# The bias of the last product enters through a gated modulation row, and ScalarE instead of VectorE empties the product's two banks

## The chip, the core and the metric

The kernel runs on one core of a Trainium2 chip. Five engines work side by side, each through its own list of instructions in order, and wait for each other on semaphores: TensorE (PE in the profile; PEld is its weight load), VectorE (DVE), ScalarE (ACT), GpSimd (POOL) and SyncE (SP), which here issues the DMAs. The metric is the device time of one launch in microseconds (us); lower is better.

## The reference

The whole is one transformer block with adaptive layer norm, over 32 batches of 512 tokens with 256 features. Cut to what matters here:

```python
mod = (silu(c) @ wmod).reshape(B, 6, 1, -1)
sa, ca, ga, sb, cb, gb = (mod[:, i] for i in range(6))
ga, gb = ((2*(g >= 0) - 1) * maximum(abs(g), 0.25) for g in (ga, gb))
h  = layernorm(x) * (1 + ca) + sa
x  = x + ga * attn_and_ssm(h)        # softmax attention + a selective scan + an FFN
h  = layernorm(x) * (1 + cb) + sb
x  = x + gb * (h @ base_w.T + base_b + 2.0 * lora_of_top2_experts(h))
```

`attn_and_ssm` is attention with 16 heads, beside it a state-space scan (512 channels times 16 states, over the 512 tokens), then an FFN with GELU. The last line is the one that the change touches: a product, a bias `base_b`, a gate `gb`, and the residual.

## The kernel before, in words

A batch of 512 tokens is four tiles of 128. The scan of a batch is 64 steps `e`, each over a 128x512 tile: ScalarE makes the decay (`dec`, L695), GpSimd fills the state (`fill`, L582), VectorE scans (`scan`, L1173), VectorE or GpSimd multiplies by C (`c`, L1181; `pc`, L569), TensorE adds it up in PSUM (`add`, L914). The states lie in a ring of eight, the rows of B and C come by DMA (`bc`, L436) into four slots. Between these stands the other work of three batches at once: the next batch's layer norm, projections and convolution (names with + in the tables), this batch's attention, the last batch's tail (names with -).

Four tables, ORDER["POOL"], ORDER["ACT"], ORDER["DVE"] and ORDER["PE"], and one for SP, write out by hand in which order each engine takes its steps in one turn of the loop. `drive` runs the table once per batch: 32 turns, the first two and last two outside the loop. Nothing is scheduled at run time: an engine waits at a step until its semaphores are there, and what stands behind waits too.

The steps that the prediction follows, in the order of one turn:

- `x2`, `x2b` on GpSimd (L623, L626): the second residual `xr` = x + ga * (...), a 128x1024 tile in SBUF. SP has loaded `xr`, the two gate rows `mod_g` (L504) and `mod_f` for it.
- `l3s` on VectorE and GpSimd, `l3a` on ScalarE (L702): the layer norm of `xr`. GpSimd then goes on with `fill27` to `fill31`, and `fill32` to `fill35` as soon as the next row of B is in.
- `ql0` to `ql3` on VectorE (L1210): the third bfloat16 part of Q and K of the next batch. Both inputs, `dbc` (the tile `qkf`) and the part before, lie in SBUF. The first two of four run beside `fill27` to `fill31`.
- `route` and `lora` on VectorE: the top-2 weights. `lora` has two small instructions with both inputs in SBUF (L1308, L1314), then L1319, from which TensorE's transposes `axt` (L923) take the lora part.
- `out0`, `out1` on TensorE (L1094, L1096): the last product, into PSUM banks 3 and 1; VectorE adds the bias row `bb_row` and writes SBUF (L1326). TensorE's `st0_3_0` needs bank 3 next, `mx1_6` bank 1.
- `mx1_4` to `mx1_10` (L1235): the maxima of attention scores on VectorE; `mx1_4` and `mx1_5` use the same bank 0, so TensorE starts `mx1_5` (L1002, L1004) when VectorE has read `mx1_4`. They end in `mt1`, whose result goes by DMA to the scores of the next group of heads.
- `gb` and `put` on GpSimd (L632, L635): times the gate row, plus `xr`.

The eviction before reads:

```python
v.tensor_tensor(nrm(b)[:, 2*n:2*n+2], pM[...] , bb_row (broadcast), ALU.add)   # DVE
nc.gpsimd.tensor_tensor(nrm(b), nrm(b), row(mod_g[:, 1, :]), ALU.mult)         # gb
nc.gpsimd.tensor_tensor(nrm(b), nrm(b), xr, ALU.add)                           # put
```

Of the kernel before, what the change touches and what calls it, by code (L numbers as in the profile page):

```python
# [1345 lines left out]
def parse(text):  # L1346
# [14 lines left out]
        fill40 fill41 pc38 fill42 fill43 pc39 fill44 fill45 fill46 fill47 fill48 fill49 fill50 fill51 pc46 pc47
        fill52 fill53 fill54 fill55 fill56 fill57 fill58 fill59 pc54 fill60 fill61 pc55 fill62 fill63 +u0 +u1
        +fill0 +fill1 pc62 pc63 +fill2 +fill3 +fill4 +fill5 +fill6 +fill7 +fill8 +fill9 +pc6 +pc7 +fill10 +fill11
        +fill12 +fill13 l2s +fill14 +fill15 +fill16 +fill17 +pc14 f1_0 +fill18 +pc15 +fill19
# [94 lines left out]
```

## Time and profile before

| | us |
|---|---|
| three runs | 6279.98, 6290.32, 6291.08 |
| their median | 6290.32 |
| the profiled execution | 6288.11, its span 6286.3 |
| VectorE busy | 5319.2 (85%) |
| TensorE busy, granted clock | 5399.8 (86%), 0.94 |
| GpSimd busy | 4141.0 (66%) |
| ScalarE busy | 4051.5 (64%) |

A turn of the loop takes 181 to 196 us. A timeline row gives the start in us from the beginning of the span, the length, the engine, the line, the operation with output and inputs, how many instructions are merged in it, and in square brackets how long the engine had been idle before and what ended that. Inputs are named once: `region<-region` may be two tiles of the region. Ends of TensorE's matmuls are modelled.

### The profile page before, as it was taken

Reading aid. Unit: us, or ns where it says so; the run is one execution under the profiler, and the core shown is the slowest. Engines: PE = TensorE matmul, PEld = TensorE weight load, DVE = VectorE, ACT = ScalarE, POOL = GpSimd, SP = SyncE. Lnnn points to the kernel's source line nnn. Section 1 sums busy time; section 2 is a strip of 40 time slices with the busy share of each in tenths; the row PEclk is TensorE's granted clock in tenths of the full one; section 3 lists DMA queues with packets and bytes.
Section 4 is the critical chain, followed back from the end, with each engine's and each line's share of the span. In section 5 each row is a group of like instructions: output and inputs, shape, how many; then the busy total and the mean of one; then the engine's idle time right before and its main releaser. Section 6 shows DMA issues by size and latency. Waiting matters only on the chain.

```text
span 6286.3 us, 116694 instructions
## 1 busy us (share of the span) xinstructions
PE 5399.8 (86%) x32280; PEld 3560.7 (57%) x32280; DVE 5319.2 (85%) x8095; ACT 4051.5 (64%) x6215; POOL 4141.0 (66%) x3409
## 2 busy tenths in 40 slices
PE   4788988888888888888888888888888989888986
PEld 2455655556555565555565555565555655555664
DVE  4888889888899888898888898888898888988883
ACT  3666766666666666766666666667766667666663
POOL 3666676667676676676666666676766666766762
PEclk7899999999999999999999999999999999999998
DMA  4443444444444444444434444434444444444331
GB/s 123 137 128 120 135 130 143 137 122 131 132 134 135 133 126 129 134 138 132 138 120 125 127 148 135 124 125 134 132 138 135 125 125 132 141 130 140 123 117 44
DMA packets 517124, 810.56 MB, mean 129 GB/s; under 512 B 79921, under 2 KB 222681, under 8 KB 516369
## 3 DMA queue, kind: packets, MB, share of 16 engines
q1 hardware_dynamic: 508464, 801.56, 41.4%
q8 instruction: 297, 4.87, 0.3%
q14 instruction: 459, 3.75, 0.2%
q10 hardware_dynamic: 7904, 0.39, 0.1%
...
## 4 chain that ended last, share of the span: by engine, by line
PE 34%; DVE 21%; issue 19%; POOL 9%; ACT 9%; DMA 5%; SPq 2%; ACTq 1%; DVEq 1%; POOLq 0%
PE pM L1065 7%; DVE pD L1173 5%; PE pY L914 5%; PE pM L1056 4%; DMA region<-mrow 4%; POOL state L582 4%; PE pM L1020 3%; DVE mx L1235 3%; ACT pD L695 3%; PE pM L1002 3%; DVE xc L1217 2%; DVE state L1173 2%; PE pM L936 2%; DVE state L1181 2%; PE pM L923 2%
## 5 line engine op out<-in xcount | busy, mean ns | idle before, releaser
L582 POOL TENSOR_TENSOR state<-scan_in,bc 128x512 f32<-128x512 f32 x2048 | 2586.0, 1287 | 894.3 <-PE pY L914 469.2
L1173 DVE TENSOR_TENSOR_SCAN pD<-pD,state 128x512 f32<-128x512 f32 x1536 | 1851.1, 1218 | 194.9 <-ACT pD L695 179.0
L695 ACT ACTIVATE pD<-scan_in,A 128x512 f32<-128x512 f32 x2048 | 1401.6, 689 | 641.8 <-DVE state L1181 547.8
L914 PE MATMUL pY<-ident,state 128*128 128x128 f32 x8192 | 1217.6, 285 | 94.8 <-DVE state L1181 72.1
L796 ACT ACTIVATE region<-pM 128x512 f32<-128x512 f32 (+1 forms) x1408 | 747.9, 555 | 639.7 <-PE pM L1022 619.2
L914 PEld LDWEIGHTS pY<-ident,state 128*128 128x128 f32 x8192 | 954.0, 147 | 286.2 <-issue 106.6
L1181 DVE TENSOR_TENSOR state<-pD,bc 128x512 f32<-128x512 f32 x1536 | 1032.5, 681 | 27.2 <-DMA bc<-bc_d 0.4
L1235 DVE TENSOR_REDUCE mx<-pM 128x1 f32<-128x512 f32 (+3 forms) x1408 | 863.9, 628 | 125.2 <-PE pM L1004 98.2
L569 POOL TENSOR_TENSOR state<-state,bc 128x512 f32<-128x512 f32 x512 | 645.6, 1272 | 390.9 <-DVE state L1173 390.0
L1020 PE MATMUL pM<-region 98*128 98x512 bf16 (+3 forms) x2048 | 594.5, 339 | 327.1 <-DMA region<-mrow 198.8
L1002 PE MATMUL pM<-region 96*128 96x512 bf16 (+3 forms) x2048 | 553.5, 316 | 166.9 <-DVE mrow L1248 44.7
L1173 DVE TENSOR_TENSOR_SCAN state<-pD,state 128x512 f32<-128x512 f32 x512 | 605.9, 1209 | 56.4 <-ACT pD L695 56.3
L1020 PEld LDWEIGHTS pM<-region 98*128 98x128 bf16 x2048 | 210.9, 103 | 641.5 <-ACT region L796 165.6
L1056 PE MATMUL pM<-region,w_f 128*128 128x512 f32 x1024 | 479.8, 606 | 21.2 <-ACT region L820 21.2
L1065 PE MATMUL pM<-w_f,scan_in 128*128 128x256 f32 x2048 | 455.7, 381 | 5.7 <-ACT scan_in L829 5.7
L1002 PEld LDWEIGHTS pM<-region 96*128 96x128 bf16 x2048 | 205.1, 101 | 438.3 <-issue 218.2
L1022 PE MATMUL pM<-identb,mask_qk 128*128 128x128 bf16 x2048 | 430.4, 237 | 0.0
L1065 PEld LDWEIGHTS pM<-w_f,scan_in 128*128 128x128 f32 x2048 | 385.3, 191 | 60.4 <-ACT scan_in L829 6.5
L936 PE MATMUL pM<-region,vt 128*17 128x512 f32 (+3 forms) x4096 | 383.8, 465 | 19.9 <-issue 18.8
L1004 PE MATMUL pM<-mask_qk,identb 128*128 128x128 bf16 x2048 | 400.0, 225 | 0.0
L611 POOL TENSOR_TENSOR scan_in<-scan_in,xc 128x1024 f32<-128x1024 f32 x64 | 149.5, 2357 | 250.2 <-DVE scan_in L1224 244.4
L1056 PEld LDWEIGHTS pM<-region,w_f 128*128 128x128 f32 x1024 | 182.0, 191 | 211.1 <-issue 165.4
...
## 6 DMA issues: line engine op xcount, KB each, us to landing
...
region<-qk_d SPq DMA_DIRECT2D x256, 64.0 KB, 2.3
...
```

The lines of the kernel that those rows point to most:

```text
L569: nc.gpsimd.tensor_tensor(slot, slot, bc[:, e // JP % BC_SLOTS, 1, :], ALU.mult).then_inc(pp_ok.sem, 1)
L582: nc.gpsimd.tensor_tensor(state[:, e % RING], us[:, parity(b), k // N * JP + e % JP, :], bc[:, k % BC_SLOTS, 0, :], ALU.mult).then_inc(b_o ...
L695: act.activation(pD[DECAY_BANK[e]][:], dts[:, parity(b), j], ACT.Exp, scale=A[:, j, n:n + 1]).then_inc(a_ok.sem, 1)
L796: act.activation(probs[kb % 2][:, h:h + heads, 0:n], pM[bank_of(name)][:, 0:heads * n].rearrange("p (h t) -> p h t", h=heads), ACT.Exp, sc ...
L914: ins = pe.matmul(y_part(t, e % JP), state[:, e % RING, t * P:(t + 1) * P], ident[:], is_transpose=True, start=False, stop=(e % PASS >= PA ...
L1002: pe.matmul(ps[:, s * n:(s + 1) * n], q[0:QK_ROWS, h, qb * P:(qb + 1) * P], kk[0:QK_ROWS, h, 0:n], start=True, stop=False, skip_group_chec ...
L1020: pe.matmul(ps[:, i * n:(i + 1) * n], kk[0:QK_ROWS + 2, h + i, kb * P:(kb + 1) * P], q[0:QK_ROWS + 2, h + i, kb * P:L], start=True, stop=F ...
L1056: ins = pe.matmul(ps[:], w_f1[:, k, f * P:(f + 1) * P], h2T[:, k], start=(k == 0), stop=(k == KT - 1))
L1065: ins = pe.matmul(ps[:, t * D:(t + 1) * D], gT(b)[:, f, (2 * n + t) * P:(2 * n + t + 1) * P], w_f2[:, f, :], start=(f == 0), stop=(f == FT ...
L1173: v.tensor_tensor_scan(h if e in POOL_C else decay, decay, h, 0.0, ALU.mult, ALU.add)\
L1181: v.tensor_tensor(state[:, e % RING], pD[DECAY_BANK[e]][:], bc[:, slot, 1, :], ALU.mult)\
L1235: v.tensor_reduce(mx[:, g % 2].rearrange("p (h q) -> p h q", q=TB)[:, heads[0]:heads[-1] + 1, qb], pM[bank_of(name)][:, 0:len(heads) * n]. ...
```

## The change

The bias is taken out of the eviction: gb * (p + base_b) = gb * p + gb * base_b. In the set-up VectorE makes gb * base_b for all 32 batches as a seventh modulation row beside the six. In each turn SP loads that row as a third of `mod_g` (one DMA more, 128 KB), and GpSimd adds it to `xr` in a new step `xb`, behind the layer norm that reads `xr`. The two evictions of the last product become plain copies on ScalarE. The tables change in four places: `-xb` behind `fill28` on GpSimd, `-out0 -out1` behind `dec33` on ScalarE, the same two names gone from VectorE; TensorE's and SP's tables stay.

```diff
-        mod_rows = dram("mod_rows", (B, 6 * D))
+        mod_rows = dram("mod_rows", (B, 7 * D))
...
-                    for a, col in ((0, 2), (1, 5)):
+                    for a, col in ((0, 2), (1, 5), (2, 6)):
                         sp.dma_start(mod_g[:, a], mod_rows[b.index, col * D:(col + 1) * D].partition_broadcast(P))\
                           .then_inc(modg_in.sem, 16)
...
+                elif name == "xb":
+
+                    b.wait(pool, n3)
+                    nc.gpsimd.tensor_tensor(xr, xr, row(mod_g[:, 2, :]), ALU.add).then_inc(xb_ok.sem, 1)
...
                 elif name == "put":
                     b.wait(pool, o_gb)
+                    b.wait(pool, xb_ok)
...
+                elif name in ("out0", "out1"):
+                    n = int(name[3])
+                    b.wait(act, out_ps, n + 1)
+                    act.activation(nrm(b)[:, 2 * n:2 * n + 2], pM[bank_of(name)][:].rearrange("p (t f) -> p t f", t=2),
+                                   ACT.Copy).then_inc(o_sum.sem, 1)
...
+            dve.wait_ge(bb_in, 16)
+            link(v.tensor_tensor(mods[0:B, 6 * D:7 * D], mods[0:B, 5 * D:6 * D], bb_row[0:B], ALU.mult))
...
-                elif name in ("out0", "out1"):
-                    n = int(name[3])
-                    b.wait(dve, out_ps, n + 1)
-                    v.tensor_tensor(nrm(b)[:, 2 * n:2 * n + 2], pM[bank_of(name)][:].rearrange("p (t f) -> p t f", t=2),
-                                    bb_row[:].unsqueeze(1).broadcast_to([P, 2, D]), ALU.add)\
-                     .then_inc(o_sum.sem, 1)
...
-        fill28 fill29 fill30 fill31 fill32 fill33 fill34 fill35 pc30 pc31 fill36 -gb fill37 -put fill38 fill39
+        fill28 -xb fill29 fill30 fill31 fill32 fill33 fill34 fill35 pc30 pc31 fill36 -gb fill37 -put fill38
...
-        dec31 st0_2_2 dec32 dec33 st0_3_0 dec34 dec35 st1_0_0 st1_0_1 dec36 st1_0_2 oe0 dec37 st1_0_3 st1_1_0
+        dec31 st0_2_2 dec32 dec33 -out0 -out1 st0_3_0 dec34 dec35 st1_0_0 st1_0_1 dec36 st1_0_2 oe0 dec37 st1_0_3
```

GpSimd, from the small instructions of the layer norm of `xr` on. Before:

```order
L549 TENSOR_TENSOR ln_rs<-ln_mv,eps 128x4
L550 TENSOR_TENSOR ln_nm<-ln_mv,mone 128x4
L552 TENSOR_TENSOR ln_rs<-ln_rs,mhalf 128x4
L555 TENSOR_TENSOR ln_nm<-ln_nm,ln_rs 128x4
L582 TENSOR_TENSOR state<-scan_in,bc 128x512 x9
L569 TENSOR_TENSOR state<-state,bc 128x512 x2
```

Changed:

```order
L551 TENSOR_TENSOR ln_rs<-ln_mv,eps 128x4
L552 TENSOR_TENSOR ln_nm<-ln_mv,mone 128x4
L554 TENSOR_TENSOR ln_rs<-ln_rs,mhalf 128x4
L557 TENSOR_TENSOR ln_nm<-ln_nm,ln_rs 128x4
L584 TENSOR_TENSOR state<-scan_in,bc 128x512 x2
L634 TENSOR_TENSOR region<-region 128x1024
L584 TENSOR_TENSOR state<-scan_in,bc 128x512 x7
L571 TENSOR_TENSOR state<-state,bc 128x512 x2
```

The 128x1024 add `xb` now stands between the second and the third of the nine fills.

VectorE, from the last instruction of `lora` to the scan of step 33. Before:

```order
L1319 TENSOR_TENSOR scan_in<-pM,top 128x512
L1181 TENSOR_TENSOR state<-pD,bc 128x512
L1173 SCALAR_TENSOR_TENSOR pD<-pD,state 128x512
L1181 TENSOR_TENSOR state<-pD,bc 128x512
L1173 SCALAR_TENSOR_TENSOR state<-pD,state 128x512 x2
L1173 SCALAR_TENSOR_TENSOR pD<-pD,state 128x512
L1326 TENSOR_TENSOR scan_in<-pM,bb_row 128x512
L1181 TENSOR_TENSOR state<-pD,bc 128x512
L1235 TENSOR_REDUCE mx<-pM 128x1
L1326 TENSOR_TENSOR scan_in<-pM,bb_row 128x512
L1235 TENSOR_REDUCE mx<-pM 128x1
L1173 SCALAR_TENSOR_TENSOR pD<-pD,state 128x512
```

Changed:

```order
L1333 TENSOR_TENSOR scan_in<-pM,top 128x512
L1195 TENSOR_TENSOR state<-pD,bc 128x512
L1187 SCALAR_TENSOR_TENSOR pD<-pD,state 128x512
L1195 TENSOR_TENSOR state<-pD,bc 128x512
L1187 SCALAR_TENSOR_TENSOR state<-pD,state 128x512 x2
L1187 SCALAR_TENSOR_TENSOR pD<-pD,state 128x512
L1195 TENSOR_TENSOR state<-pD,bc 128x512
L1249 TENSOR_REDUCE mx<-pM 128x1 x2
L1187 SCALAR_TENSOR_TENSOR pD<-pD,state 128x512
```

The two evictions are gone, and the maxima `mx1_4` and `mx1_5` follow one another directly.

ScalarE, from the eviction of `axt`. Before:

```order
L841 ACTIVATE scan_in<-pM 128x512
L695 ACTIVATE pD<-scan_in,A 128x512
L796 ACTIVATE region<-pM 128x2x256
L695 ACTIVATE pD<-scan_in,A 128x512
L796 ACTIVATE region<-pM 128x2x256
L695 ACTIVATE pD<-scan_in,A 128x512 x2
L796 ACTIVATE region<-pM 128x4x128
L695 ACTIVATE pD<-scan_in,A 128x512 x2
```

Changed:

```order
L853 ACTIVATE scan_in<-pM 128x512
L702 ACTIVATE pD<-scan_in,A 128x512
L803 ACTIVATE region<-pM 128x2x256
L702 ACTIVATE pD<-scan_in,A 128x512
L803 ACTIVATE region<-pM 128x2x256
L702 ACTIVATE pD<-scan_in,A 128x512 x2
L849 ACTIVATE scan_in<-pM 128x512 x2
L803 ACTIVATE region<-pM 128x4x128
L702 ACTIVATE pD<-scan_in,A 128x512 x2
```

The two evictions stand ahead of the exponential of `st0_3_0` (128x4x128).

## Rows read from the trace of the kernel before

**Rows 1.** Busy us by stretch: one turn, from `x2b` to L1319, and its rest.
```profile
core 0: us, PE busy (x) PEld busy (x) DVE busy (x) ACT busy (x) POOL busy (x), PEclk, DMA share, GB/s
2843.90:2867.80 23.90, 20.86 (x114) 12.25 (x113) 20.19 (x43) 13.03 (x24) 12.37 (x12) 1.00 0.47 154
2867.80:3031.40 163.60, 145.15 (x895) 97.92 (x896) 145.86 (x210) 113.31 (x171) 116.83 (x96) 0.95 0.42 131
```

**Rows 2.** Timeline of VectorE around the two evictions, in that turn.
```profile
2873.06 1.21 DVE L1173 TENSOR_TENSOR_SCAN pD<-pD,state 128x512 f32<-128x512 f32 x1
2874.18 0.67 DVE L1326 TENSOR_TENSOR scan_in<-pM,bb_row 128x512 f32<-128x512 f32 x1
...
2875.83 0.68 DVE L1326 TENSOR_TENSOR scan_in<-pM,bb_row 128x512 f32<-128x512 f32 x1
2876.42 0.55 DVE L1235 TENSOR_REDUCE mx<-pM 128x1 f32<-128x384 f32 x1
```

**Rows 3.** Timeline of TensorE there: end of `out1`, then `mx1_5`.
```profile
2874.98 0.59 PE L1096 MATMUL pM<-w_lb,scan_in 128*128 128x256 f32 x2
2875.96 0.34 PE L1002 MATMUL pM<-region 96*128 96x384 bf16 x1 [0.39 <-DVE mx L1235]
2876.14 0.22 PE L1004 MATMUL pM<-mask_qk,identb 128*128 128x128 bf16 x1
```

**Rows 4.** Timeline of ScalarE there: the exponential of `st0_3_0`.
```profile
2877.22 0.60 ACT L796 ACTIVATE region<-pM 128x512 f32<-128x512 f32 x1 [3.35 <-PE pM L1022]
```

**Rows 5.** Timeline of ScalarE at `l3a`, same turn.
```profile
2850.31 1.57 ACT L702 ACTIVATE scan_in<-region,ln_nm,ln_rs 128x256 f32<-128x256 f32 x3
```

**Rows 6.** Timeline of GpSimd, same turn: `fill28`, `fill32` to `fill35`, `gb`.
```profile
2850.96 1.72 POOL L582 TENSOR_TENSOR state<-scan_in,bc 128x512 f32<-128x512 f32 x1
...
2866.32 4.98 POOL L582 TENSOR_TENSOR state<-scan_in,bc 128x512 f32<-128x512 f32 x4 [9.51 <-DMA bc<-bc_d]
...
2879.68 2.35 POOL L632 TENSOR_TENSOR scan_in<-scan_in,region 128x1024 f32<-128x1024 f32 x1
```

**Rows 7.** Timeline of VectorE, same turn: `ql0`, `ql1`, `ql2`, `ql3`, end of `lora`.
```profile
2849.91 1.64 DVE L1210 TENSOR_TENSOR qkp<-dbc,qkp 128x512 bf16<-128x512 f32 x1
...
2854.71 0.97 DVE L1210 TENSOR_TENSOR ht<-dbc,ht 128x512 bf16<-128x512 f32 x1 [0.19 <-ACT ht L743]
...
2858.17 0.68 DVE L1210 TENSOR_TENSOR qkp<-dbc,qkp 128x512 bf16<-128x512 f32 x1
...
2865.44 0.68 DVE L1210 TENSOR_TENSOR ht<-dbc,ht 128x512 bf16<-128x512 f32 x1
...
2867.75 0.69 DVE L1319 TENSOR_TENSOR scan_in<-pM,top 128x512 f32<-128x512 f32 x1
```

**Rows 8.** Timeline of GpSimd in another turn: `fill32`.
```profile
2292.07 1.57 POOL L582 TENSOR_TENSOR state<-scan_in,bc 128x512 f32<-128x512 f32 x1 [8.88 <-DMA bc<-bc_d]
```

**Rows 9.** Timeline of VectorE in the turn of rows 8: `ql3` and `lora`.
```profile
2291.82 0.68 DVE L1210 TENSOR_TENSOR ht<-dbc,ht 128x512 bf16<-128x512 f32 x1
2292.42 1.27 DVE L1308 TENSOR_TENSOR top<-top,keep 128x32 f32<-128x32 f32 x1
...
2294.16 0.76 DVE L1314 SCALAR_TENSOR_TENSOR top<-top,esum 128x32 f32<-128x32 f32 x1
2295.02 0.69 DVE L1319 TENSOR_TENSOR scan_in<-pM,top 128x512 f32<-128x512 f32 x1
```

**Rows 10.** Two lines of VectorE, whole span: busy us, mean ns | idle before.
```profile
L1314 DVE SCALAR_TENSOR_TENSOR top<-top,esum 128x32 f32<-128x32 f32 x32 | 25.6, 801 | 1.1
...
L1308 DVE TENSOR_TENSOR top<-top,keep 128x32 f32<-128x32 f32 x32 | 10.4, 324 | 3.9 <-ACT top L838 3.9
```

**Rows 11.** Timeline of SP: the two gate rows of a turn.
```profile
3014.35 0.87 SPq L504 DMA_DIRECT2D region<-mod_rows  x2
```

**Rows 12.** Timeline of GpSimd: `x2` of that turn.
```profile
3028.94 2.36 POOL L623 TENSOR_TENSOR scan_in<-x,region 128x1024 f32<-128x1024 f32 x1 [7.13 <-DVE x L1283]
```

**Rows 13.** Who waited for SP's DMA of the split parts (L456): us, times.
```profile
  ACT qkp L738: 6.9, 5
```

More of the change, by code:

```diff
@@ L215, in adaln_block @@
         lns = [stats_tiles(f"ln{n}") for n in range(4)]
-        REGION = 12288
+        REGION = 12544
         region = sb("region", [P, REGION])
@@ L239, in adaln_block @@
         xr = view(TB * D).rearrange("p (t f) -> p t f", t=TB)
-        mod_g = view(2 * D).rearrange("p (a f) -> p a f", a=2)
+        mod_g = view(3 * D).rearrange("p (a f) -> p a f", a=3)
         def gT(b):
@@ L265, in adaln_block @@
         rt_raw = view(D)
-        mods = view(6 * D)
+        mods = view(7 * D)
+        bb_row = view(D)
         alpha = view(D)
@@ L345, in adaln_block @@
         la_ps, ax_ok, axt_ps, axt_ok = sig("la_ps", 1), sig("ax_ok", 1), sig("axt_ps", 1), sig("axt_ok", 1)
+        xb_ok = sig("xb_ok", 1)
         out_ps, o_sum, o_gb, o_fin, out_done = (sig("out_ps", 2), sig("o_sum", 2), sig("o_gb", 1),
@@ L409, in _ @@
             load(A[:], d["A_log"].rearrange("(j p) n -> p j n", p=P))
-            for row, name in ((ob_row, "o_b"), (f2b_row, "ffn_b2"), (bb_row, "base_b"), (rb_row, "router_b")):
+            for row, name in ((ob_row, "o_b"), (f2b_row, "ffn_b2"), (rb_row, "router_b")):
                 load(row[:], d[name].partition_broadcast(P))
@@ L1335 @@
              + [(1, [0, 1]), (1, [2, 3]), (0, [0, 1, 2, 3])])
-N_LOADS = 39
+N_LOADS = 38
 ACT_LOADS = 22
@@ L1339 @@
 BUILT = 11
-MODS_READY = 14
+MODS_READY = 15
 MODS_DONE = MODS_READY + 1
@@ L1359 @@
         +l0s fill20 fill21 +l0a fill22 +l0b fill23 +l0c fill24 +l1s fill25 pc22 fill26 pc23 -x2 -x2b -l3s fill27
-        fill28 fill29 fill30 fill31 fill32 fill33 fill34 fill35 pc30 pc31 fill36 -gb fill37 -put fill38 fill39
[L1361 to L1364, printed above, removed]
+        fill28 -xb fill29 fill30 fill31 fill32 fill33 fill34 fill35 pc30 pc31 fill36 -gb fill37 -put fill38
+        fill39 fill40 fill41 pc38 fill42 fill43 pc39 fill44 fill45 fill46 fill47 fill48 fill49 fill50 fill51 pc46
+        pc47 fill52 fill53 fill54 fill55 fill56 fill57 fill58 fill59 pc54 fill60 fill61 pc55 fill62 fill63 +u0
+        +u1 +fill0 +fill1 pc62 pc63 +fill2 +fill3 +fill4 +fill5 +fill6 +fill7 +fill8 +fill9 +pc6 +pc7 +fill10
+        +fill11 +fill12 +fill13 l2s +fill14 +fill15 +fill16 +fill17 +pc14 f1_0 +fill18 +pc15 +fill19
     """,
@@ L1396 @@
         mx1_0 +l1s scan23 scan24 c24 scan25 -f2_0 scan26 -f2_1 c25 -l3s +qk0 mx1_1 +ql0 mx1_2 scan27 +qk1 c26
-        +ql1 +qk2 scan28 c27 +ql2 mx1_3 -route +xs0 +qk3 +xs1 +ql3 -lora c28 scan29 c29 scan30 scan31 scan32
-        -out0 c32 mx1_4 -out1 mx1_5 scan33 mx1_6 c33 mx1_7 mx1_8 mx1_9 mx1_10 mt1 scan34 mx2_0 gate0 c34 scan35
-        c35 scan36 scan37 c36 mx2_1 c37 on0 scan38 scan39 mx2_2 scan40 mx2_3 c40 scan41 mx2_4 scan42 c41 c42
-        mx2_5 mx2_6 +xs2 mx2_7 mx2_8 mx2_9 mx2_10 scan43 mt2 c43 +xs3 scan44 mx3_0 scan45 mx3_1 c44 mx3_2 on1 c45
-        mx3_3 scan46 scan47 mx3_4 scan48 c48 mx3_5 scan49 scan50 mx3_6 c49 mx3_7 c50 mx3_8 scan51 scan52 c51
-        mx3_9 mx3_10 c52 mt3 scan53 c53 scan54 +mx0_0 scan55 scan56 scan57 c56 c57 scan58 scan59 c58 c59 on2 +sp3
-        scan60 c60 scan61 c61 scan62 scan63 +scan0 +scan1 +c0 +c1 on3 gate1 +scan2 +c2 +scan3 +scan4 +c3 +c4
-        +scan5 +c5 +scan6 +scan7 +scan8 +c8 +scan9 +c9 +scan10 +c10 sso0 +scan11 +c11 sso1 l2s +scan12 +scan13
-        +c12 +mx0_1 +mx0_2 +c13 +scan14 +mx0_3 +scan15 +mx0_4 +scan16 +c16 +scan17
+        +ql1 +qk2 scan28 c27 +ql2 mx1_3 -route +xs0 +qk3 +xs1 +ql3 -lora c28 scan29 c29 scan30 scan31 scan32 c32
+        mx1_4 mx1_5 scan33 mx1_6 c33 mx1_7 mx1_8 mx1_9 mx1_10 mt1 scan34 mx2_0 gate0 c34 scan35 c35 scan36 scan37
+        c36 mx2_1 c37 on0 scan38 scan39 mx2_2 scan40 mx2_3 c40 scan41 mx2_4 scan42 c41 c42 mx2_5 mx2_6 +xs2 mx2_7
+        mx2_8 mx2_9 mx2_10 scan43 mt2 c43 +xs3 scan44 mx3_0 scan45 mx3_1 c44 mx3_2 on1 c45 mx3_3 scan46 scan47
+        mx3_4 scan48 c48 mx3_5 scan49 scan50 mx3_6 c49 mx3_7 c50 mx3_8 scan51 scan52 c51 mx3_9 mx3_10 c52 mt3
+        scan53 c53 scan54 +mx0_0 scan55 scan56 scan57 c56 c57 scan58 scan59 c58 c59 on2 +sp3 scan60 c60 scan61
+        c61 scan62 scan63 +scan0 +scan1 +c0 +c1 on3 gate1 +scan2 +c2 +scan3 +scan4 +c3 +c4 +scan5 +c5 +scan6
+        +scan7 +scan8 +c8 +scan9 +c9 +scan10 +c10 sso0 +scan11 +c11 sso1 l2s +scan12 +scan13 +c12 +mx0_1 +mx0_2
+        +c13 +scan14 +mx0_3 +scan15 +mx0_4 +scan16 +c16 +scan17
     """,
```

16 lines of the change are left out of this document (8 added, 8 removed).

## The prediction

> **What bounds the kernel now.** I read the busy times by stretch first. From `x2b` to the end of `lora` a turn has VectorE busy for 20.19 of 23.90 us, and in the rest for 145.86 of 163.60 us; TensorE has as much [rows 1]. Neither is the bound alone: each waits now for the other. So the next view is the timeline of both where the change cuts. VectorE goes from the scan of step 32 to the first eviction, on to `mx1_4`, the second eviction and `mx1_5` without a pause [rows 2], and TensorE waits 0.39 us for VectorE's `mx1_4` before it can start `mx1_5` [rows 3]. ScalarE has 3.35 us of idle time before `st0_3_0` [rows 4]. GpSimd has 9.51 us before `fill32`, in which it waits for a row of B [rows 6]. Taken by idle time alone the change looks free: work leaves the engine that is waited for and goes to two that are waiting. The view that says otherwise is the length of single VectorE instructions while GpSimd works, below.
>
> **What leaves VectorE.** Two evictions, 0.67 and 0.68 us long, the next instruction 0.59 us behind the start [rows 2]: 1.2 us a turn, on an engine without a pause there. Not all of it is won. Without them the product of step 32 starts when its scan ends, 2873.06 + 1.21 = 2874.3, `mx1_4` about 0.6 later at 2874.9, and it ends (0.55 long, like `mx1_5`) at 2875.45. But `mx1_5` uses the same bank, and TensorE is in `out1` until 2875.5 to 2875.6 (2874.98 + 0.59 is the modelled end [rows 3]). So TensorE becomes the late one: `mx1_5` starts there at 2875.55 and is complete 0.40 us later (2876.14 + 0.22 - 2875.96), and VectorE reads it at 2875.95 instead of 2876.42 [rows 2, 3]. **The gain is 0.5 us a turn**; the other 0.7 us becomes a wait of VectorE for TensorE. From there to `mt1` VectorE has no slack, so the 0.5 us should reach the scores of the next heads: 30 turns x 0.5 = **15 us**.
>
> **What ScalarE gets.** Two copies of a 128x512 bank, by the eviction in rows 4 about 0.6 us each. The first bank is full long before, the second at 2875.57, so the second copy ends near 2876.2. TensorE's `st0_3_0`, which was complete shortly before 2877.22, comes 0.45 us earlier, at about 2876.75. So both copies lie in the 3.35 us of idle time and cost nothing; were the cover gone, one copy would cost 0.6 us a turn, 18 us in all. Behind them stand that exponential and the decays of steps 34 and 35, which VectorE reads some us later.
>
> **What SP gets.** One more DMA issue, 0.87 / 2 = 0.43 us, at 3015.2, and SP's later `mod_f` as much later. GpSimd's `x2` starts at 3028.94, and the last thing that it waited for was VectorE [rows 11, 12]. Even a landing 10 us after issue comes before that: nothing. In the set-up one small VectorE product of 32x256 is added and one DMA moves forward: between 0.2 us (a 32-wide instruction less its stall) and 0.7 us (a 512-wide one, rows 7), I take 0.5 us, once.
>
> **What GpSimd gets.** `xb` is a 128x1024 add, 2.35 us like `gb` [rows 6]. It waits for `l3a`, which ends at 2850.31 + 1.57 = 2851.9, before `fill28` ends at 2852.68 [rows 5, 6]: no wait. What is queued behind it are `fill29` to `fill31`, each 2.3 us later; nobody needs them early (`scan29` comes after `lora`), and `fill32` still waits for its DMA. On GpSimd's own account: nothing.
>
> Now the same turn with `xb`: it starts at 2852.64 and ends at 2854.99. `ql1`, asked for at 2854.71, ends at 2855.54 (before: 2855.68). `fill29` is held by it until 2855.54 + 1.14 = 2856.68, and fills follow at 1.24 us ((4.98 - 1.27) / 3 in rows 6, with 1.27 for one alone): `fill30` from 2856.64 and `fill31` from 2857.88 to 2859.15. `ql2` comes at 2858.17 [rows 7], when before the fills had been over for 1.4 us (`fill31` began at 2855.09). It is now held, and ends at 2859.15 + 0.55 = 2859.70 instead of 2858.85: **+0.85 us**. From here to L1319 VectorE is back to back, and so it hands this on.
>
> That delay brings `ql3` from 2865.44 to 2866.3, where `fill32` starts at 2866.32, set by a DMA that the delay doesn't touch. This is the pattern of [rows 8, 9]: there L1319 starts 3.20 us after `ql3`, here it was 2.31 [rows 7, 9]. On average before, L1308 and L1314 lose 0.14 and 0.61 us (324 and 801 less 0.18 and 0.19 unheld) = 0.75; in the pattern 1.09 + 0.57 = 1.66 us: **+0.9 us**. Together 1.75 us a turn. It holds for the turns in which `ql2` comes while `fill31` runs, I count 26 of 30; in the others Q's first DMA landed late (ScalarE waited for it five times [rows 13]), and `ql2` comes after the fills even now. 26 x 1.75 = 45 us. In some turns `fill32` starts just before `ql3`; then `ql3` is held too and L1319 loses another 1.15 us; I take four such turns, 5 us. **The loss is 50 us.** Ends: 26 x 0.85 = 22 us if only `ql2` is hit, 26 x 2.9 = 75 us if `fill32` is always first.
>
> The Trainium skill states this as a rule (SBUF — State Buffer, "Who interferes with whom"): a VectorE instruction with two SBUF inputs and a GpSimd instruction that reads SBUF need one shared port pair, and the one that comes second waits for the whole instruction. By that rule, the trace agrees: 1.64 against 0.68 us. By a rule in which GpSimd costs VectorE nothing the sum would be 6288 - 15.
>
> **The sum.** 6288.1 (the profiled execution) - 15 + 50 + 0.5 = 6323.6. The median of the runs is 2.2 above the profiled execution: **6325 us** (rounded).
>
> **Rivals.**
> (a) The meeting of `ql2` and `fill31` doesn't happen or is made up later. For it: it hangs on an offset of 0.3 us into `fill31`, and TensorE and ScalarE have idle time too. Against it: the turns repeat to a few hundredths, and VectorE shows no pause until `mt1`. Then only the gain is left: 6290 - 15 = 6275. It decides as soon as `ql2` comes 1 us later than now.
> (b) The whole 1.2 us is won and nothing is lost, because TensorE's modelled end of `out1` is too late: 6290 - 30 x 1.2 = 6254.
> (c) Only the first meeting costs, since `lora` finds `fill32` elsewhere: 6290 - 15 + 22 = 6297, no change.
> (d) TensorE's longer wait ahead of `axt` (it follows L1319) costs clock as well. The granted clock is 1.00 in the stretch before and 0.95 over the rest [rows 1]; were it half in the 7 us from `axt` to `out1`, each turn would lose up to 3.5 us, 100 us at most; I put one turn in five at half of that, 10 us, in the range and not in the sum. With it and (c)'s upper end: over 6350.
> (e) The change doesn't do what it says, since ScalarE, now in VectorE's place, is late for the banks: it has `dec33` in front, which waits for the scan of step 31. That scan ends before the one of step 32, so a copy can't start later than VectorE's did; even then 6290.
>
> **How the numbers follow.** Chances: the forecast (6303 to 6350) 0.60, (a) 0.12, (b) 0.04, (c) 0.14, (d) above 6350 0.06, (e) 0.04. Range: from (a), 6273, to 6350; (b) and (d) are left out. About 0.2% (12.6 us) is what a measurement of this kernel can tell from no change. Faster by more: (a) and (b), 0.16; within: (c) and (e), 0.18; slower: 0.66.
>
> **What would show it.** In the changed profile the third L1210 of a turn takes about 1.6 us instead of 0.68 in most turns; L1308's mean rises from 0.32 towards 1.2 us; L1326's line is gone and VectorE waits about 0.6 us for TensorE before `mx1_5`; ScalarE's idle time before `st0_3_0` shrinks; `xb` starts right behind `fill28`. If the third L1210 is still 0.68 us long, the loss isn't there and the time is (a)'s. If it is 1.6 and the time is still no more than before, the delay was made up behind `lora`, and my step from VectorE's timeline to the span is wrong.

## The result and the profile after

| | before | changed |
|---|---|---|
| median of the runs, us | 6290.7 (6279.98 to 6305.84, 6 runs) | 6351.03 (6336.21 to 6366.26, 6 runs) |
| profiled execution, its span | 6288.11, 6286.3 | 6349.76, 6348.0 |
| ratio of changed to before, 95% interval | | 1.0097 [1.0078, 1.0116] |

The changed kernel is slower by 60 us (49 to 73 by the interval), where 35 were forecast. The direction and the main mechanism were right, the size was not, and the time lies 1 us above the range.

First the groups of instructions of VectorE in the changed kernel: line, operation, out<-in, count | busy us, mean ns of one | idle before, and who ended it. L1224 is L1210 of before, L1322 and L1328 are L1308 and L1314, L1333 is L1319, L1249 is L1235, L584 is L582, L634 is the new `xb`.

```profile
L1249 DVE TENSOR_REDUCE mx<-pM 128x1 f32<-128x384 f32 x512 | 275.0, 542 | 46.9 <-PE pM L1016 25.8 <-issue 20.3
...
L1224 DVE TENSOR_TENSOR qkp<-dbc,qkp 128x512 bf16<-128x512 f32 x64 | 98.7, 1542 | 1.4 <-ACT qkp L750 1.4
...
L1322 DVE TENSOR_TENSOR top<-top,keep 128x32 f32<-128x32 f32 x32 | 35.2, 1100 | 3.8 <-ACT top L845 3.8
...
L1328 DVE SCALAR_TENSOR_TENSOR top<-top,esum 128x32 f32<-128x32 f32 x32 | 23.5, 734 | 1.1
```

The same groups of before:

```profile
L1235 DVE TENSOR_REDUCE mx<-pM 128x1 f32<-128x384 f32 x512 | 274.4, 541 | 23.7 <-issue 19.8 <-PE pM L1004 3.1
...
L1210 DVE TENSOR_TENSOR qkp<-dbc,qkp 128x512 bf16<-128x512 f32 x64 | 73.0, 1141 | 1.4 <-ACT qkp L743 1.4
```

Half of the `qkp` instructions are `ql0`, which stays at 1.65 us; the other half, `ql2`, went up: 64 x (1542 - 1141) / 32 = 0.80 us more a turn. L1322 went from 324 to 1100 ns, L1328 from 801 to 734 [rows 10]. And in front of the 384-wide maxima, `mx1_5` among them, VectorE now waits 25.8 us for TensorE instead of 3.1.

Now one turn of the changed kernel, the same as that of [rows 2 to 7]. GpSimd, from `fill27` to `fill31`:

```profile
2889.89 2.95 POOL L584 TENSOR_TENSOR state<-scan_in,bc 128x512 f32<-128x512 f32 x2
2892.80 2.36 POOL L634 TENSOR_TENSOR region<-region 128x1024 f32<-128x1024 f32 x1
2895.12 4.17 POOL L584 TENSOR_TENSOR state<-scan_in,bc 128x512 f32<-128x512 f32 x3
```

VectorE at the same time: `ql1`, and `ql2`:

```profile
2894.88 0.83 DVE L1224 TENSOR_TENSOR ht<-dbc,ht 128x512 bf16<-128x512 f32 x1 [0.20 <-ACT ht L750]
...
2898.26 1.58 DVE L1224 TENSOR_TENSOR qkp<-dbc,qkp 128x512 bf16<-128x512 f32 x1
```

`xb` starts right behind `fill28`. The fills are over at 2895.12 + 4.17 = 2899.29, and `ql2`, asked for at 2898.26, ends at 2899.84, 0.55 us behind them. It was 0.68 us long in [rows 7]. Then GpSimd's `fill32` and VectorE's `ql3` and `lora`:

```profile
2906.30 2.94 POOL L584 TENSOR_TENSOR state<-scan_in,bc 128x512 f32<-128x512 f32 x2 [7.01 <-DMA bc<-bc_d]
```

```profile
2906.43 1.68 DVE L1224 TENSOR_TENSOR ht<-dbc,ht 128x512 bf16<-128x512 f32 x1
2908.03 1.25 DVE L1322 TENSOR_TENSOR top<-top,keep 128x32 f32<-128x32 f32 x1
...
2909.76 0.75 DVE L1328 SCALAR_TENSOR_TENSOR top<-top,esum 128x32 f32<-128x32 f32 x1
2910.61 0.69 DVE L1333 TENSOR_TENSOR scan_in<-pM,top 128x512 f32<-128x512 f32 x1
```

Here `fill32` is 0.13 us before `ql3`: the worse of the two patterns of the prediction, in which `ql3` is held as well. L1333 starts 26.56 us behind `x2b` (at 2884.05); before it was 23.9 [rows 1, 7].

What follows in this turn, TensorE:

```profile
2911.36 0.66 PE L935 MATMUL pM<-ident,scan_in 128*128 128x128 f32 x4 [2.65 <-DVE scan_in L1333]
...
2913.15 1.91 PE L1106 MATMUL pM<-w_base,region 128*128 128x256 f32 x4
...
2917.12 1.08 PE L1106 MATMUL pM<-w_base,region 128*128 128x256 f32 x4
```

The second and the third row are four matmuls each, of one shape, in `out0` and in `out1`: they take 1.91 us the first time and 1.08 the second. Busy us by stretch, from `x2b` to L1333 and from there to `mt1`; the granted clock stands behind the parenthesis of POOL:

```profile
core 0: us, PE busy (x) PEld busy (x) DVE busy (x) ACT busy (x) POOL busy (x), PEclk, DMA share, GB/s
2884.05:2910.62 26.57, 21.13 (x114) 12.18 (x113) 22.79 (x43) 12.95 (x24) 17.39 (x14) 1.00 0.48 150
2910.62:2925.80 15.18, 13.71 (x100) 11.01 (x101) 12.75 (x18) 7.27 (x12) 7.31 (x6) 0.89 0.18 51
```

Behind a wait of 2.65 us, TensorE ran for 3.4 us of the second stretch at 1.2 GHz, half of its 2.4 (0.11 lost of 15.18 us is 1.7, so 3.4 at half). This is rival (d).

To see where 62 us of span go, I took the start of `x2b`, of L1319 (L1333) and of `mt1` from the timelines of all 28 turns between the first two and the last two, and made the means. They are of one execution of each kernel:

| us a turn | before | changed | difference | forecast |
|---|---|---|---|---|
| `x2b` to L1319 | 24.00 | 25.77 | +1.77 | +1.67 (50 / 30) |
| L1319 to `mt1` | 14.19 | 14.06 | -0.13 | -0.50 |
| `mt1` to the next `x2b` | 152.21 | 152.65 | +0.44 | 0 |
| whole turn | 190.40 | 192.48 | +2.08 | +1.17 |

30 turns x 2.08 = 62 us, the whole difference of the two spans. The loss was well sized; most of the gain is missing, and the stretch behind `mt1` came on top. How far that last row can be trusted is said further down.

### The profile page after: what moved, and what is told of

The parts are those of the page before. It is cut to its first block, busy times and chain, and to the rows that moved or that the text cites. A ratio compares the mean times of both kernels' runs of the same rounds, so it can differ in the third digit from the quotient of the medians.

```text
span 6348.0 us, 116848 instructions
## 1 busy us (share of the span) xinstructions
PE 5417.2 (85%) x32280; PEld 3571.8 (56%) x32280; DVE 5341.6 (84%) x8032; ACT 4086.0 (64%) x6279; POOL 4224.2 (67%) x3441
## 4 chain that ended last, share of the span: by engine, by line
PE 36%; DVE 19%; issue 19%; POOL 9%; ACT 9%; DMA 5%; SPq 2%; ACTq 1%; DVEq 0%; POOLq 0%
PE pM L1077 7%; PE pY L926 5%; PE pM L1068 4%; DVE pD L1187 4%; POOL state L584 4%; DMA region<-mrow 4%; PE pM L1032 3%; PE pM L1014 3%; DVE xc L1231 2%; ACT pD L702 2%; DVE mx L1249 2%; PE pM L948 2%; PE pM L1106 2%; DVE state L1187 2%; DVE state L1195 2%
## 5 line engine op out<-in xcount | busy, mean ns | idle before, releaser
L584 POOL TENSOR_TENSOR state<-scan_in,bc 128x512 f32<-128x512 f32 x2048 | 2596.0, 1291 | 864.1 <-PE pY L926 534.9
L1249 DVE TENSOR_REDUCE mx<-pM 128x1 f32<-128x512 f32 (+3 forms) x1408 | 864.6, 629 | 145.3 <-PE pM L1016 117.1
```

The costliest lines, as they stand in the source:

```text
L584: nc.gpsimd.tensor_tensor(state[:, e % RING], us[:, parity(b), k // N * JP + e % JP, :], bc[:, k % BC_SLOTS, 0, :], ALU.mult).then_inc(b_o ...
L1249: v.tensor_reduce(mx[:, g % 2].rearrange("p (h q) -> p h q", q=TB)[:, heads[0]:heads[-1] + 1, qb], pM[bank_of(name)][:, 0:len(heads) * n]. ...
```

## The experiments

All ratios are to the kernel before, run on the same chip beside them, with 95% intervals. Its median there was 6288.82 us for e1 to e4, 6290.93 for e5 to e8 and 6290.23 for e9 to e11, so kernels of different groups are compared by their ratios. "Changed" is the kernel of the diff. Times of a part of the turn are means of 28 turns, worked out as in the table above.

**Each half of the change alone.** The first kernel is the kernel before with ScalarE in VectorE's place for the two evictions; there is no bias, no `xb` and no seventh row. The second is the changed kernel with the evictions back on VectorE, as copies.

```diff
# e1, against before
-        dec31 st0_2_2 dec32 dec33 st0_3_0 dec34 dec35 ...
+        dec31 st0_2_2 dec32 dec33 -out0 -out1 st0_3_0 dec34 dec35 ...
-        -out0 c32 mx1_4 -out1 mx1_5 scan33 ...
+        c32 mx1_4 mx1_5 scan33 ...
# e2, against changed
-        dec31 st0_2_2 dec32 dec33 -out0 -out1 st0_3_0 dec34 dec35 ...
+        dec31 st0_2_2 dec32 dec33 st0_3_0 dec34 dec35 ...
-        ... scan31 scan32 c32 mx1_4 mx1_5 scan33 ...
+        ... scan31 scan32 -out0 c32 mx1_4 -out1 mx1_5 scan33 ...
```

> The kernel before with one part of the change: ScalarE evicts the last product, behind dec33, as a plain copy. No seventh row, no xb; the bias is left out of the computation. Theory A (the changed kernel is slower only because GpSimd's xb makes the fills meet VectorE's third L1210): L1319 stays at 24.0 us behind x2b, the stretch from L1319 to mt1 is 0.36 us shorter as in the changed kernel, and the time is 6291 - 30 x 0.36 = 6280. Theory B (the 0.45 us a turn that came behind mt1 are ScalarE's doing): the stretch from mt1 to the next x2b is longer by that, and the time is 6290 or more.

> The changed kernel with the evictions given back to VectorE, as plain copies at their old places; the seventh row, its DMA and xb stay. Theory A: the third L1210 takes 1.58 us, L1319 comes 1.77 us later, nothing is won behind it: 6291 + 30 x 1.77 = 6344, and if what came behind mt1 is a consequence of the delay too, up to 6365. Theory B: 6344 or less, and the stretch behind mt1 is as in the kernel before.

Measured: e1 6279.77 us, ratio 0.9992 [0.9982, 1.0001], with 13.83 us from L1319 to `mt1` instead of 14.19; e2 6356.21 us, 1.0117 [1.01, 1.0134], with 25.96 us from `x2b` to L1319 instead of 24.00, and with 14.67 us from there to `mt1`, since 11 of its 28 turns are at half clock there. VectorE in e2:

```profile
L1219 DVE TENSOR_TENSOR qkp<-dbc,qkp 128x512 bf16<-128x512 f32 x64 | 99.3, 1552 | 1.4 <-ACT qkp L750 1.4
...
L1317 DVE TENSOR_TENSOR top<-top,keep 128x32 f32<-128x32 f32 x32 | 36.6, 1143 | 3.8 <-ACT top L845 3.8
```

All of the loss comes with `xb`, all of the gain with the evictions. And the gain is 0.36 us a turn, 11 us, not 15. In the time of the whole kernel it isn't clear of noise: e1's interval reaches 1.

**`xb` out of VectorE's way, or VectorE out of `xb`'s.** e3 is the changed kernel with `xb` behind `pc31`; e4 leaves `xb` where it is and puts `ql2` behind `mx1_3` and `route`, after the fills; e7 puts `xb` behind `fill31`, so that `ql2` meets `xb` itself and not a fill.

```diff
# e3, against changed
-        fill28 -xb fill29 fill30 fill31 fill32 fill33 fill34 fill35 pc30 pc31 fill36 -gb ...
+        fill28 fill29 fill30 fill31 fill32 fill33 fill34 fill35 pc30 pc31 -xb fill36 -gb ...
# e4, against changed
-        ... scan28 c27 +ql2 mx1_3 -route +xs0 ...
+        ... scan28 c27 mx1_3 -route +ql2 +xs0 ...
# e7, against changed
-        fill28 -xb fill29 fill30 fill31 fill32 ...
+        fill28 fill29 fill30 fill31 -xb fill32 ...
```

> The changed kernel with xb moved on GpSimd's table from behind fill28 to behind pc31, ahead of fill36, where GpSimd waited 3.9 us for TensorE and VectorE reads PSUM. Theory A: the third L1210 is 0.68 us again, L1319 at 24.0 us, gain of 0.36 us a turn kept: 6280. Rival (any 2.3 us of added GpSimd work costs, since GpSimd is late for the ring behind it): fill36 and what follows come later, the scans of steps 36 to 38 wait, and it stays above 6300.

> The changed kernel with one swap on VectorE's table: the third L1210 (ql2) stands behind mx1_3 and route instead of ahead of them, so it is asked for about 1.6 us later, when fill31 is over; GpSimd's order stays as changed. Theory A: it takes 0.68 us, L1319 is back at about 24.0 us, and the time is 6280. Rival (the fills that come 2.3 us later hurt by themselves, whatever VectorE meets): still about 6350.

> The changed kernel with xb behind fill31 instead of behind fill28. No fill is late any more, but xb itself now runs from 12.9 to 15.2 us behind x2b, when the third L1210 comes at 14.3. Theory A (what counts is only that GpSimd is reading SBUF when VectorE asks for two SBUF inputs): the third L1210 takes 1.6 us, L1319 comes 1.7 us late, 6350. Rival (what counts is that the fills are late): 0.68 us and 6280.

Measured: e3 6278.02 us, 0.9988 [0.9974, 1.0002]; e4 6281.96 us, 0.9996 [0.9983, 1.0009]; e7 6350.46 us, 1.0092 [1.0075, 1.0108]. In the turn of the traces above `ql2` is short in e3 and e4 and held in e7. First e3:

```profile
2861.83 0.68 DVE L1224 TENSOR_TENSOR qkp<-dbc,qkp 128x512 bf16<-128x512 f32 x1
```

Then e4, where it stands behind the `route` instructions:

```profile
2868.15 0.68 DVE L1224 TENSOR_TENSOR qkp<-dbc,qkp 128x512 bf16<-128x512 f32 x1
```

And e7, GpSimd's `xb` and VectorE's `ql2`:

```profile
2890.33 2.35 POOL L634 TENSOR_TENSOR region<-region 128x1024 f32<-128x1024 f32 x1
```

```profile
2891.73 1.50 DVE L1224 TENSOR_TENSOR qkp<-dbc,qkp 128x512 bf16<-128x512 f32 x1
```

`xb` ends there at 2892.68 and `ql2` at 2893.23, 0.55 us behind it, just as behind a fill. So what costs isn't `xb`'s time on GpSimd, its DMA or its place in a queue; it is that `ql2` is asked for while GpSimd adds, be it a fill or `xb`. e4 has exactly the GpSimd work of the changed kernel and is faster by 1.0097 - 0.9996 = 1.0%, 63 us, by one name that moved on VectorE. And with `ql2` free, L1308's mean stays near before's too (357 ns in e3, 404 in e4, against 1100): the second meeting, of `lora` with `fill32`, is a consequence of the first.

**Does it take a read?** e11 is e3 with a `memset` of GpSimd on an unused 128x2048 bfloat16 view of `x1` behind `fill31`, so that `ql2` meets an instruction that writes SBUF and reads nothing. SP's next load of `x1` waits for the memset.

```diff
# e11, against e3
-                    b.wait_last(sp, x2_ok, 1)
+                    b.wait_last(sp, ms_ok)
                     sp.dma_start(x1[:], hres_d[b.index].rearrange("(t p) f -> p t f", p=P)).then_inc(x1p_in.sem, 16)
...
+                elif name == "ms":
+                    nc.gpsimd.memset(x1_f.bitcast(BF16), 0.0).then_inc(ms_ok.sem, 1)
-        fill28 fill29 fill30 fill31 fill32 ...
+        fill28 fill29 fill30 fill31 -ms fill32 ...
```

> The kernel with xb behind pc31, and a GpSimd memset of 128x2048 bfloat16 (about 1.8 us, into a dead tile) behind fill31: it writes SBUF and reads nothing, and runs from 12.9 to 14.7 us behind x2b, when the third L1210 comes at 14.3. Theory A (only GpSimd's reading of SBUF holds a VectorE instruction with two SBUF inputs): the third L1210 stays at 0.68 us, and the time is that without the memset, 6278. Rival (any GpSimd instruction that uses SBUF holds it): it takes about 0.95 us, and L1319 comes 0.3 to 1.2 us later, 6290 to 6315.

Measured: 6288.13 us, 0.9995 [0.9983, 1.0007]. GpSimd and VectorE in the same turn:

```profile
2855.80 1.81 POOL L638 MEMSET x<- 128x2048 bf16 x1
```

```profile
2857.22 0.68 DVE L1228 TENSOR_TENSOR qkp<-dbc,qkp 128x512 bf16<-128x512 f32 x1
```

The memset runs until 2857.61, `ql2` is asked for at 2857.22 and takes its 0.68 us. Had it been held, it would have ended at 2857.61 + 0.55 = 2858.16; it ends at 2857.90. In 29 turns `ql2` starts during the memset, and their mean is 0.68 us. The Trainium skill states this limit (SBUF — State Buffer, "Who interferes with whom"): a two-input VectorE instruction contends with a GpSimd instruction that reads SBUF, and not with one that only writes. By that rule, the trace agrees. The overlap here is only the last 0.4 us of the memset; an overlap with its start wasn't tried. The time of the kernel doesn't decide between the two theories: its median is 10 us above e3's, near the rival's 6290, but the intervals of the two ratios overlap (e3's is 0.9974 to 1.0002). The length of `ql2` decides it.

**Why the gain is 0.36 us and not more.** The prediction let `mx1_5` wait for the end of `out1`. e5 was to make `out1` earlier: it lets TensorE do `st0_2_2` and `add27` before `axt`, in the time in which it waits for L1333 anyway. e6 does the same to the changed kernel, e8 to the kernel before. e9 instead lets VectorE do other work between `mx1_4` and `mx1_5`.

```diff
# e5 against e3, e6 against changed, e8 against before
-        ... pv0_0 pv0_1 -axt st0_2_2 add27 -out0 mx1_4 -out1 mx1_5
+        ... pv0_0 pv0_1 st0_2_2 add27 -axt -out0 mx1_4 -out1 mx1_5
# e9, against e3
-        ... scan31 scan32 c32 mx1_4 mx1_5 scan33 mx1_6 c33 ...
+        ... scan31 scan32 mx1_4 c32 scan33 mx1_5 mx1_6 c33 ...
```

> The changed kernel with xb behind pc31 and, on TensorE's table, st0_2_2 and add27 moved from behind axt to ahead of it, where TensorE waits for L1319 (0.80 us on average). It tests why only 0.36 of the 1.2 us of the evictions is won. Theory A (TensorE's chain axt, st0_2_2, add27, out0, out1 is what mx1_5 then waits for): with 0.85 us less in that chain, the stretch from L1319 to mt1 shrinks from 13.83 to 13.2 us, and the time is 6278 - 30 x 0.6 = 6260. Rival (VectorE's chain itself, through c32 and the maxima, allows no more): it stays at 6278.

> The changed kernel, xb left behind fill28, with the same swap on TensorE's table alone. TensorE's wait ahead of axt falls from 1.86 us on average to 1.0. Theory A (in five of 28 turns a wait of more than about 2.4 us there took the clock down for out0 and out1, which cost 1.3 to 1.5 us each): no turn between L1319 and mt1 at half clock any more, 0.23 us a turn, and 0.6 us from the shorter chain: 6351 - 30 x 0.8 = 6327. Rival: the swap gives only the 0.6 us, and the half clock stays: 6333.

> The kernel before with the swap on TensorE's table alone. Theory A: before, VectorE is the later one at mx1_5 (out1 was complete 0.26 us ahead of the second eviction), so a TensorE that is 0.85 us earlier wins nothing: 6289. Rival (TensorE's chain sets the pace there in any case): 6289 - 30 x 0.6 = 6271.

> The changed kernel with xb behind pc31, and on VectorE's table scan32 mx1_4 c32 scan33 mx1_5 in place of scan32 c32 mx1_4 mx1_5 scan33. The run before this one showed that a TensorE 0.85 us earlier changes nothing there: VectorE waits 0.49 us for mx1_5 either way. Theory A: that wait is the way of bank 0 from VectorE's reading of mx1_4 to TensorE's refill and back, and a 1.2 us scan in between hides it, with the 0.12 us that c32 waited for its scan: L1319 to mt1 shrinks from 13.83 to about 13.25 us, the time from 6278 to 6260. Rival (the wait moves to mx1_7, which needs bank 0 too, or to mt1): 13.8 us and 6278.

Measured: e5 6292.29 us, 1.0005 [0.9996, 1.0014]; e6 6334.81 us, 1.0069 [1.0049, 1.0088]; e8 6304.16 us, 1.0019 [1.001, 1.0028]; e9 6280.49 us, 0.9983 [0.9972, 0.9994]. First VectorE in e3, from `scan32` on:

```profile
2876.72 1.20 DVE L1187 TENSOR_TENSOR_SCAN pD<-pD,state 128x512 f32<-128x512 f32 x1
2878.04 0.69 DVE L1195 TENSOR_TENSOR state<-pD,bc 128x512 f32<-128x512 f32 x1
2878.65 0.55 DVE L1249 TENSOR_REDUCE mx<-pM 128x1 f32<-128x384 f32 x1
2879.69 0.56 DVE L1249 TENSOR_REDUCE mx<-pM 128x1 f32<-128x384 f32 x1 [0.49 <-PE pM L1016]
```

Then the same in e5:

```profile
2881.19 1.21 DVE L1187 TENSOR_TENSOR_SCAN pD<-pD,state 128x512 f32<-128x512 f32 x1
2882.52 0.69 DVE L1195 TENSOR_TENSOR state<-pD,bc 128x512 f32<-128x512 f32 x1
2883.13 0.55 DVE L1249 TENSOR_REDUCE mx<-pM 128x1 f32<-128x384 f32 x1
2884.16 0.56 DVE L1249 TENSOR_REDUCE mx<-pM 128x1 f32<-128x384 f32 x1 [0.49 <-PE pM L1016]
```

VectorE's wait of 0.49 us is the same, but this doesn't clear `out1`, because `out1` is no earlier in e5. TensorE's wait before `axt` is down from 0.80 to 0.16 us, and a new one stands behind `axt`, for ScalarE's eviction of it (L853):

```profile
2877.99 1.13 PE L1106 MATMUL pM<-w_base,region 128*128 128x256 f32 x4 [0.69 <-ACT scan_in L853]
...
2883.12 0.59 PE L1108 MATMUL pM<-w_lb,scan_in 128*128 128x256 f32 x2
```

The last matmuls of `out1` start 2883.12 - 2881.19 = 1.93 us behind the scan in e5, and 1.90 in e3 (2878.62 below, less 2876.72). The same 0.69 us stand in e6 and e8, which therefore don't test `out1` either. The chain from L1333 over `axt` and ScalarE's eviction to `out0` is as long with the swap as without.

In e3, VectorE reads `mx1_4` until 2878.65 + 0.55 = 2879.20, and only then TensorE refills bank 0:

```profile
2878.62 0.59 PE L1108 MATMUL pM<-w_lb,scan_in 128*128 128x256 f32 x2
2879.26 0.34 PE L1014 MATMUL pM<-region 96*128 96x384 bf16 x1
2879.43 0.22 PE L1016 MATMUL pM<-mask_qk,identb 128*128 128x128 bf16 x1
```

The modelled end of `out1` is at 2879.21, so these rows alone don't tell which of the two held the refill. e9 does. There VectorE reads `mx1_4` right behind the scan, then does `c32` and the next scan:

```profile
2876.72 0.53 DVE L1249 TENSOR_REDUCE mx<-pM 128x1 f32<-128x384 f32 x1
...
2878.90 0.53 DVE L1249 TENSOR_REDUCE mx<-pM 128x1 f32<-128x384 f32 x1
2879.72 0.56 DVE L1249 TENSOR_REDUCE mx<-pM 128x1 f32<-128x384 f32 x1 [0.29 <-PE pM L1016]
...
2881.61 1.29 DVE L1249 TENSOR_REDUCE mx<-pM 128x2 f32<-128x512 f32 x2 [0.27 <-PE pM L1016]
```

And TensorE in e9:

```profile
2877.51 0.59 PE L1108 MATMUL pM<-w_lb,scan_in 128*128 128x256 f32 x2
2877.94 0.33 PE L1014 MATMUL pM<-region 96*128 96x384 bf16 x1
```

The bank is free there from 2877.25 on, and `mx1_5` starts 2877.94 - 2877.51 = 0.43 us behind `out1`'s last matmuls. In e3 it starts 2879.26 - 2878.62 = 0.64 us behind them. So in e3 the bank's way back is what ends last, by 0.21 us; the other 0.28 of VectorE's 0.49 us would have been waited for `out1` in any case.

In e9 `mx1_5` no longer waits, but `mx1_6` and a later one wait 0.29 and 0.27 us for TensorE. L1319 to `mt1` is 13.62 us, against 13.83 in e3. The time of the whole kernel doesn't show this: e9 is faster than before by 0.17% with an interval clear of 1, but e3's interval covers the same ratio. e5's median is 6292 where both of its theories said 6278 or less, and e8 is slower than before, clear of noise, though nothing was added to it; no run shows why.

**What the clock takes.** e10 is the changed kernel with twelve needless 128x128 transposes on TensorE ahead of `axt`, into the bank that `st0_2_2` fills next. All else stays, `xb` and the held `ql2` too.

```diff
# e10, against changed
-        ... pv0_0 pv0_1 -axt st0_2_2 add27 -out0 ...
+        ... pv0_0 pv0_1 -busy -axt st0_2_2 add27 -out0 ...
```

> The changed kernel with 12 needless transposes of the identity on TensorE ahead of axt, into the bank that st0_2_2 fills next: they keep TensorE at work where it waits 1.67 to 2.7 us for L1319. Theory A (the clock fell because of that wait): no turn at half clock between L1319 and mt1, this stretch 13.83 us in all turns instead of 14.06 on average; 0.23 us a turn, 6344. Rival (the half clock there has another cause): five or so of 28 turns still have it.

Measured: 6360.28 us, 1.0109 [1.009, 1.0128]. TensorE in a turn, and the stretch from L1333's counterpart to `mt1`:

```profile
2901.12 1.53 PE L1102 MATMUL pM<-ident 128*128 128x128 f32 x12
2903.65 0.66 PE L935 MATMUL pM<-ident,scan_in 128*128 128x128 f32 x4 [0.99 <-DVE scan_in L1338]
```

```profile
2902.90:2916.73 13.83, 12.31 (x100) 9.61 (x100) 12.73 (x17) 7.19 (x12) 7.25 (x5) 1.00 0.20 57
```

In all 28 turns the clock is 1.00 and the stretch 13.8 or 13.9 us long. In the four other kernels in which `ql2` is held, 25 of 112 turns have the half clock: 5 each in the changed kernel and e7, 11 in e2, 4 in e6. So filling TensorE's idle time ahead of `axt` with work takes the half clock away, and the half clock costs 14.06 - 13.83 = 0.23 us a turn in the changed kernel, 7 us in all (0.48 us a turn in e2). e6 doesn't contradict this: its wait before `axt` is halved, 0.92 us against 1.86, but with the 0.69 us behind `axt` TensorE idles 1.61 us there, and the half clock stays (0.49 us a turn against 0.61). The 7 us that e10 was to win didn't reach the end. Its trace lost 0.22 us a turn ahead of L1333, where `fill32` came before `ql3` in 14 turns instead of 10, and 0.22 behind `mt1`; its interval overlaps the changed kernel's.

The means of all kernels, in us a turn, each from one execution, beside the median of the runs:

| | `ql2` | wait before `axt` | to L1319 | at half clock | to `mt1` | to next `x2b` | median, us |
|---|---|---|---|---|---|---|---|
| before | 0.68 | 0.79 | 24.00 | 0.00 | 14.19 | 152.21 | 6290.7 |
| changed | 1.53 | 1.86 | 25.77 | 0.61 | 14.06 | 152.65 | 6351.03 |
| e1 | 0.68 | 0.91 | 24.00 | 0.00 | 13.83 | 151.97 | 6279.77 |
| e2 | 1.55 | 2.04 | 25.96 | 1.34 | 14.67 | 151.83 | 6356.21 |
| e3 | 0.68 | 0.80 | 23.89 | 0.00 | 13.83 | 152.11 | 6278.02 |
| e4 | 0.68 | 0.80 | 23.98 | 0.09 | 13.84 | 152.39 | 6281.96 |
| e5 | 0.68 | 0.16 | 23.99 | 0.00 | 13.89 | 152.75 | 6292.29 |
| e6 | 1.55 | 0.92 | 25.68 | 0.49 | 14.05 | 152.21 | 6334.81 |
| e7 | 1.38 | 1.67 | 25.63 | 0.61 | 14.06 | 152.65 | 6350.46 |
| e8 | 0.68 | 0.11 | 24.07 | 0.00 | 14.24 | 152.57 | 6304.16 |
| e9 | 0.68 | 0.90 | 24.09 | 0.00 | 13.62 | 152.58 | 6280.49 |
| e10 | 1.58 | 0.62 | 25.99 | 0.00 | 13.83 | 152.87 | 6360.28 |
| e11 | 0.68 | 0.76 | 23.88 | 0.00 | 13.83 | 152.23 | 6288.13 |

"At half clock" is the time at 1.2 GHz between L1319 and `mt1`. "Wait before `axt`" is TensorE's; in e5, e6 and e8 another 0.69 us follow behind `axt`.

## Why the prediction came out too low

**What leaves VectorE: right idea, 0.14 us a turn too big.** The forecast was 0.5 us a turn; undisturbed turns gave 0.36 (e1, e3). Of the 1.2 us, the prediction saw that 0.7 would be turned into a wait, and put the wait down to `out1` alone. The product of step 32 doesn't start when its scan ends but 0.12 us later (2878.04 against 2876.72 + 1.20 in e3), a gap that the first eviction had covered. That makes the read of `mx1_4` later, and with it bank 0's way back, which e9 shows to be what ends last. The maximum `mx1_5` is read 8.29 us behind L1333 in e3; the forecast had 8.20 (2875.95 less 2867.75).

**ScalarE's copies: right.** In e3 the second copy waits 1.22 us for TensorE, and the exponential behind it starts as soon as `st0_3_0` is there:

```profile
2877.46 0.58 ACT L849 ACTIVATE scan_in<-pM 128x512 f32<-128x512 f32 x1
2879.25 0.60 ACT L849 ACTIVATE scan_in<-pM 128x512 f32<-128x512 f32 x1 [1.22 <-PE pM L1108]
2880.23 0.60 ACT L803 ACTIVATE region<-pM 128x512 f32<-128x512 f32 x1 [0.38 <-PE pM L1034]
```

**SP's DMA, the set-up, `xb` on GpSimd's own account: right, as far as can be measured.** e3 carries them all and is at 0.9988 of before; e1, which has none of them, is at 0.9992.

**GpSimd's new place: right, each step nearly to the number.** `ql2` is held in 27 of 28 turns (26 of 30 were forecast). In 26 of them it takes about 1.58 us, 0.90 more than before, against 0.85 forecast; once it takes 0.90. L1308 rose to 1.10 us ("towards 1.2"). `fill32` is before `ql3` more often than in the four turns that I took: in 10 of 28, by up to 0.7 us, and in each of them L1333 starts 25.97 to 26.76 us behind `x2b` instead of 25.56. In two turns L1322 wasn't held and L1333 came at 24.45. The sum is 1.77 us a turn against 1.67. With this (a) and (b), in which nothing is lost, and (c), in which only the first meeting costs, are out; and (e) is, since the copies came in time.

**The clock: the rival (d) that was left out of the sum.** The forecast and (d) were written as if one of them would happen. They happen together: the later L1319 is what lengthens TensorE's wait. The wait before `axt` is 1.86 us on average instead of 0.79, and in 5 of 28 turns, all of them with a wait of 2.07 to 2.70 us, TensorE is then at 1.2 GHz for 3.4 us. That costs up to 1.5 us in such a turn and 0.23 on average: 7 us, close to the 10 that the prediction put down and then did not add. With it the sum would have been 6335. The number of such turns is not a fixed price: e2, with the same `xb`, has 11.

**Behind `mt1`: not foreseen, and not settled.** +0.44 us a turn, 13 us, came from a stretch in which the change does nothing but move GpSimd's and ScalarE's work by some us. The prediction took this part as rigid, without a row for it. It isn't: in one execution of the kernel before it goes from 147.4 to 157.7 us from turn to turn. A mean of 28 such turns is known to 0.3 to 0.4 us (standard error), a difference of two of them to about 0.5, so +0.44 can't be told from nothing. The 25 executions of the kernel before beside e1 to e4 lie up to 36 us apart, 1.2 us a turn (6274.56 to 6310.11), further than the traces of all kernels do in this column (151.83 to 152.87). e2 and the changed kernel have the same `xb` and the same held `ql2`, and differ there by 0.82 us. TensorE is at half clock for 17.3 to 18.5 us a turn behind `mt1`, but that doesn't follow the length either (e8 has the least, 17.3, and 152.57 us). The medians say a little more: of their 60 us (49 to 73) the two parts ahead of `mt1` make (1.77 - 0.13) x 30 = 49, which leaves 0 to 24 for the rest. Whether the change causes any of that stays open.

**The step that failed** is the sum. It took two terms as nothing that weren't shown to be nothing: TensorE's clock, which (d) had priced at 10 us and which measured 7, and everything behind `mt1`, 13 us in the trace. Both had the sign of the loss. Its gain was 15 us where 11 were measured, its loss 50 where 53 were. In the traces that is 4 us of gain that wasn't there, 3 more of loss ahead of L1319, 7 of clock and 13 behind `mt1`, 27 together: the 62 us of the spans less the 35 forecast. With the gain, the loss and the clock as measured the sum would have been near 6340, inside the range; what put the time outside is the part that stays open. That it ended 1 us outside and not inside is chance, since the interval of the difference is 24 us wide. (The last addition also slipped: 6323.6 + 2.2 is 6325.8, not 6325.) A range for this kernel should have had room for some 15 us of such scatter.
